# A 32-sample two-layer linear/softmax attention kernel: layer 0's query product as four full-array matmuls into one PSUM bank, and a new order of all pieces

## Chip, cores and metric

The kernel runs on one core of one Trainium2 chip. The metric is the device time of one execution in microseconds (us); lower is better. Times of one kernel in several runs agree within about 0.1%.

## What is computed

The reference takes x of shape (32, 256, 256) and a condition vector per sample, and applies two conditioned attention layers, one after the other. All 32 samples are independent. In short:

```
layer 0 (8 heads of 32):
  xn = ln(x);  q = softmax(xn @ Wq + bq, over the 32 features of a head)
  k  = softmax(xn @ Wk + bk + mask, over the 256 tokens);  v = (xn @ Wv + bv) * mask
  att = k^T v   (32 x 32 per head);   y = q @ att   (per head)
  x  = x + silu(ln(y) * (1 + scale) + shift) @ W_out + b_out
layer 1 (16 heads of 16):
  ordinary softmax(q k^T) v attention with the same wrapping
```

The change touches `y = q @ att` of layer 0, called the query product here. `att` is block-diagonal over heads: of a 128 x 128 block of features (four heads), only the four 32 x 32 blocks on the diagonal are not zero.

## The kernel before

The work of one sample ("batch" b) is cut into some 60 kinds of pieces, a function each, such as `k0(b)`, `y0(b)`, `rows(b, u)`. Each of the five queues (PE, DVE, ACT, POOL, and SP for DMA) has its pieces written out by hand in one fixed order: 1275 pieces on PE, 1025 on DVE, 884 on ACT, 740 on POOL and 398 on SP. Samples overlap: PE works on `k0` of sample 20 while `cols` of 13 and `pv` of 12 are under way. An engine takes its pieces strictly in the order of its list, so a piece whose input is late holds up what stands behind it. Every piece ends in an increment of a semaphore, on which its users wait.

PSUM has 8 banks. The table `BANK` gives each group of results (`gq0`, `gy0`, `gr3`, ...) a home bank for each sample, and the table `FREED` names what a piece must wait for before it may write there. Matmuls on 64-row halves of the array run in pairs into two neighbouring banks, `n` and `n + 1`; `n` is then even. That holds for `rows` and `cols` (layer 1's scores, each 128 x 1024), `ty`, the transposes `ktT`, `qtT`, `y0T`, `y1T`, and, before the change, `y0`.

The pieces around the change, for sample b: `att` (PE, L771) makes the 32 x 32 blocks; `at_` (ACT, L1712) copies them into the tile `AT`, which is zeroed once by a memset (L2131), so that what is off the diagonal stays zero; `qt` (ACT, L1702) fills `QTs`; `y0` (PE, L784) multiplies; `rq` (DVE, L1244) makes reciprocals of the softmax sums; `Y0` (DVE, L1259) scales the product into `Y`; `s1` (DVE, L1188) takes statistics; `n1` (ACT), `r1` and `yn0` (POOL, L1989) normalise; `y0T` (PE, L718) transposes. Before the change a matmul of `y0` covers two heads, 64 rows of the array, so `AT` is only 64 columns wide, and features of the even and the odd pairs of heads land in two different banks. `Y` holds them in that order, and `yn0` puts them right as it writes.

Before the pieces run as a pipeline there is a set-up: loads of weights (`ld_w0`, `ld_f0`, `ld_w1`, ...), scales derived from their maxima (`w0m`, `w0p`), biases folded with matmuls over the whole array (`bb0`, `bb1` L976 and L978, `row3` L965 and L967), the condition's product `fx0` (L1002) and its turning `fm0` (L1009), and splits of each weight into a high and a low part in fp16 (`wh_*`, `wl_*`). On SP, `z0T(b)` (L525) turns the normalised input of sample b for PE; `mbd0` (L650) writes out the mask rows, for which it waits on DVE's `mb0`.

fp32 operands are multiplied in two passes, so one fp32 matmul of the program is two records of the trace.

Of the kernel before, what the change touches and what calls it, by code (L numbers as in the profile page):

```python
# [29 lines left out]
    "gpm": "1",  # L30
    "gt_w0": "0",
    "ga_w0": "0",
    "gcnd": "2",
    "gbb1": "3",
    "grow3": "4",
    "gt_o0": "0",
    "gbb0": "5",
    "gfx0": "2",
    "gq0": "00107411307003666226230345451347",
    "gfm0": "1",  # L40
    "gk0": "25515623626142177267061266500466",
    "gv0": "34246532232453342672373552017557",
    "gt_f0": "1",
    "gkt": "66224040400000624004646204204622",
    "gqt": "62622460642604640446040222406004",
    "gat": "05300311721547046360624675464663",
    "ga_o0": "5",
    "gy0": "26260644062664226044242606002020",
    "ga_f0": "4",
    "grw": "0",  # L50
    "gt_w1": "1",
    "gy0T": "26666464424220640642622624200062",
    "ga_w1": "4",
    "gcol": "5",
    "go0": "31221232543347226263557464035354",
    "gt_b": "0",
    "ga_b": "0",
    "gbb2": "2",
    "gq1": "05703334432467473624461600242452",
    "gfx1": "1",  # L60
    "gk1": "74032224522573323734465711442453",
    "gfm1": "1",
    "gv1": "00073326407633312247747627634533",
    "gt_f1": "1",
    "gt_o1": "7",
    "gr0": "62640666660046044460000626666266",
    "gr1": "26406622042420402460420664600244",
    "gr2": "62240660406406460006204640242046",
    "gr3": "44660200622066066462204264666600",
    "gr4": "42622226400002604406600624002266",  # L70
    "gr5": "64242260404022404020202242606042",
    "gr6": "46004620622664406600226004620006",
    "gr7": "64660264402400600004242062406644",
    "ga_o1": "6",
    "gc0": "22646004044004260040040406004022",
    "gc1": "44400662600460460246224606600664",
    "ga_f1": "2",
    "gc2": "44046262024626242602460040026022",
    "gc3": "66440240246444206626224424664446",
    "gc4": "46602060602600262206204606200022",  # L80
    "gpv0": "13225522566372725565651352543201",
    "gc5": "42440266024424002246222404266066",
    "gpv1": "10604533672363434474740342452314",
    "gc6": "40260606424020260062024666624442",
    "gpv2": "06714521672272437545647223543415",
    "gc7": "20446244460420004002260400600226",
    "gpv3": "02305266532717037446757722422512",
    "gty": "04620062000044466064462002644644",
    "gy1T": "40666042444266640062604440660666",
    "go1": "23552057726271557471227354230111",  # L90
# [5 lines left out]
    "gpm": "-",  # L96
    "gt_w0": "hot",
    "ga_w0": "mx_w0",
    "gcnd": "-",
    "gbb1": "-",  # L100
    "grow3": "-",
    "gt_o0": "w0p",
    "gbb0": "-",
    "gfx0": "csT",
    "gq0": (
        "mx_o0 q1:1 mx_f0 perm qt:3 kt:5 Y0:5 at:7 qa:5 max:31 yt:11 yt:16 exp:41 exp:48 yt:28 yt:32 yt:35 Y0:16 "
        "max:102 at:19 st1:12 yt:54 yt:60 yt:64 st1:16 yt:71 yt:75 yt:79 Y0:27 max:190 exp:185 v:32 "),
    "gfm0": "mc",
    "gk0": (
        "fy0 bc0 at:2 mx_w1 bm Y0:4 max:2 exp:1 max:21 yt:8 yt:10 at:11 yt:19 yt:24 st1:6 vt:11 max:83 q1:18 Y0:17 "  # L110
        "yt:48 at:20 at:21 exp:120 yt:61 at:24 Y0:24 at:26 max:174 Y0:27 at:29 at:30 at:31 "),
    "gv0": (
        "bc1 p3 st0:1 w1p qt:3 kt:5 at:6 film1 exp:9 max:29 at:10 st0:9 yt:20 q1:14 x1:12 st1:7 st1:8 exp:84 Y0:17 "
        "max:110 st1:12 ka:18 st0:20 max:141 st1:16 st0:23 exp:153 max:174 yt:84 yt:88 exp:185 exp:191 "),
    "gt_f0": "f0m",
    "gkt": (
        "- qt:1 v:3+x1:1 bc2+at:3 v:4+ke:5 at:5+mx_f1 qt:6 yt:3+yt:2 max:25 q1:10+max:31 exp:26 exp:36 exp:45 qt:13 "
        "Y1:7 exp:68 max:91 qt:17 max:104 qt:19 exp:107 Y1:14 exp:125 exp:131 exp:137 exp:150 max:170 max:178 Y1:21 "
        "qt:29 Y1:23 exp:196 "),
    "gqt": (  # L120
        "kt:1 Y0:1 st0:2 Y0:3 qt:4 max:7 max:15 max:23 max:32 exp:27 Y1:4 max:57 Y1:6 max:72 exp:69 exp:73 Y1:10 "
        "exp:94 max:111 kt:21 max:128 Y1:15 max:144 exp:138 v:26+st0:23 exp:155 at:27+q1:28 exp:173 Y1:22 exp:187 "
        "st0:29 st1:24 "),
    "gat": (
        "q1:2 o0p kt:3 qa:1 vt:1 max:2 q1:7 kt:8 max:28 max:38 yt:15 yt:17 x1:10 Y0:13 max:75 exp:72 max:95 max:98 "
        "max:108 max:116 st1:13 st0:20 max:141 max:148 Y0:24 kt:26 yt:78 yt:83 yt:87 max:196 exp:191 Y0:31 "),
    "ga_o0": "ke:2",
    "gy0": (
        "ke:1+v:1 kt:2 kt:4 st0:3 kt:6 max:10 exp:7 max:27 max:36 exp:31 max:50 qt:12 max:68 max:74 max:84 exp:79 "
        "max:100 exp:95 max:115 exp:110 exp:119 max:138 exp:134 max:157 exp:149 exp:158 max:181 qt:28 exp:182 qt:30 "  # L130
        "max:211 max:218 "),
# [12 lines left out]
    "gt_b": "q1:4",
    "ga_b": "mx_b",
    "gbb2": "kt:3",
    "gq1": (
        "fcs v:6 max:8 vt:3 exp:9 x1:7 o:2 ka:8 ke:13 x1:11 exp:59 x1:13 vt:12 exp:84 exp:90 exp:98 ka:17 x1:19 "
        "at:22 ka:20 ka:21 ka:22 exp:153 x1:25 ke:29 x1:27 o:22 ka:28 ka:29 vt:29 ka:31 o:27 "),
    "gfx1": "x1:2",  # L150
    "gk1": (
        "q1:5 q1:6 vt:2 ke:8 x1:6 o:1 v:11 v:12 v:13 o:5 qa:11 o:7 o:8 vt:13 max:102 v:20 v:21 o:13 v:23 vt:19 q1:25 "
        "ke:26 ke:27 o:19 q1:29 exp:179 q1:31 exp:195 yt:100 qa:30 vt:30 vt:31 "),
    "gfm1": "fy1",
    "gv1": (
        "at:4 Y0:5 ka:3 max:21 v:10 yt:12 max:46 max:56 st0:11 st1:6 exp:63 q1:17 yt:40 yt:45 max:110 yt:52 yt:55 "
        "qa:19 at:23 yt:68 o:17 yt:76 ka:24 max:183 max:190 yt:92 ke:32 at:32 st1:25 yt:107 max:237 yt:115 "),
# [26 lines left out]
    "gr6": (
# [2068 lines left out]
```

## Time and profile before

| | |
|---|---|
| median of 3 runs | 807.55 us (807.45 to 808.08) |
| the profiled execution's own time | 807.33 us |
| its span, first to last instruction | 805.6 us |
| mean granted TensorE clock | 0.985 |
| instructions | 29123 |

The profiled execution took 1.73 us more than its span (807.33 - 805.6); that part is outside of all that the profile shows. Busy times are sums over the span of each engine's instructions. For PE they are read with care: ends of matmuls are modelled, and a short gap between two matmuls is covered by the first one's modelled tail. What PE could do in the time is better read from where matmuls start.

### The profile page before, as it was taken

The numbers are of one execution on the slowest core, as the hardware profiler recorded it, in microseconds if no ns is written. First come the engines' busy times: TensorE is split into PE (matmuls) and PEld (weight loads), VectorE is DVE, ScalarE is ACT, GpSimd is POOL, SyncE is SP. The second block draws the span as 40 slices with busy tenths as digits, with TensorE's granted clock in tenths as the row PEclk, the third lists the DMA queues.
The fourth block names the chain that finished last, engine by engine and source line by source line (L and its number), as shares of the span: only waits on it lengthen the run. The fifth ranks groups of instructions, "written<-read, shape, count | busy, mean of one in ns | idle before, by whom it ended". The sixth has DMA issues, their size and how long they took to land. (4 is left out here: it accounts for less than half of the span.)

```text
span 805.6 us, 29123 instructions
## 1 busy us (share of the span) xinstructions
PE 772.6 (96%) x10431; PEld 538.0 (67%) x10431; DVE 710.9 (88%) x1392; ACT 701.6 (87%) x1658; POOL 681.8 (85%) x1085
## 2 busy tenths in 40 slices
PE   7999889999999999999999999999999999999985
PEld 3575765777777677777677767777677776656542
DVE  7698899999999899998899889999889989989953
ACT  2266768899999999999999999999999999999995
POOL 7379998989999999998899998998989988897334
PEclk8799999999999999999999999999999999999998
DMA  6423544444443544355653445444544363354301
GB/s 179 91 48 80 139 115 117 103 104 121 101 125 95 126 110 105 88 146 100 126 127 92 132 89 123 111 109 89 143 115 120 72 119 91 85 148 115 110 20 53
DMA packets 149283, 86.22 MB, mean 107 GB/s; under 512 B 87404, under 2 KB 141802, under 8 KB 149130
## 3 DMA queue, kind: packets, MB, share of 16 engines
q1 hardware_dynamic: 149140, 84.36, 43.1%
q8 instruction: 84, 1.38, 0.8%
q14 instruction: 59, 0.48, 0.2%
HBM read 39.64 MB, written 25.80 MB: 81 GB/s over the span
## 5 line engine op out<-in xcount | busy, mean ns | idle before, releaser
L1301 DVE TENSOR_REDUCE NM<-banks 128x4 f32<-128x1024 f32 x256 | 306.7, 1213 | 23.3 <-PE banks L832 21.0
L1783 ACT ACTIVATE wraw<-banks 128x1024 f32<-128x1024 f32 x154 | 157.2, 1038 | 8.5 <-PE banks L845 7.7
L1985 POOL TENSOR_TENSOR rs<-ve,nhalf 128x2 f32<-128x2 f32 x128 | 89.8, 703 | 32.9 <-ACT ve L1656 31.7
L1783 ACT ACTIVATE PX<-banks 128x1024 f32<-128x1024 f32 x102 | 104.0, 1034 | 5.5 <-PE banks L845 4.6
L832 PE MATMUL banks<-SK,SQ 51*128 51x256 f16 x1024 | 96.1, 272 | 3.6 <-DMA SK<-scr 1.2
L701 PE MATMUL banks<-wo,SH 128*128 128x256 f16 x768 | 95.5, 274 | 4.2 <-POOL SH L2073 4.2
L845 PE MATMUL banks<-SQ,SK 53*128 53x256 f16 x1024 | 96.8, 272 | 1.7 <-DVE NM L1301 1.1
L701 PE MATMUL banks<-wv,ZT 128*128 128x256 f16 x768 | 95.3, 275 | 0.9 <-DVE un L1436 0.8
L2073 POOL TENSOR_TENSOR SH<-ST,SH 128x512 f16<-128x512 f32 x64 | 74.5, 1166 | 23.7 <-ACT SH L1747 20.0
L858 PE MATMUL banks<-wraw,V 128*32 128x256 f32 x1232 | 87.7, 385 | 0.7 <-ACT PX L1783 0.3
L2010 POOL TENSOR_TENSOR ZHL<-Z,ZHL 128x256 f16<-128x256 f32 x128 | 83.1, 670 | 2.6
L701 PEld LDWEIGHTS banks<-wo,SH 128*128 128x128 f16 x768 | 71.7, 98 | 19.9 <-POOL SH L2073 5.8
L701 PEld LDWEIGHTS banks<-wv,ZT 128*128 128x128 f16 x768 | 72.2, 98 | 16.0 <-issue 6.7
L2101 POOL TENSOR_TENSOR AB<-R,AB 128x512 f16<-128x512 f32 x64 | 74.6, 1172 | 6.5 <-ACT AB L1763 6.3
L1734 ACT ACTIVATE TH<-banks,hB,hA 128x256 f32<-128x256 f32 x128 | 65.6, 569 | 10.4 <-PE banks L718 7.9
L1989 POOL TENSOR_SCALAR Z<-X,nm,rs 128x256 f32<-128x256 f32 x128 | 69.7, 553 | 4.5 <-issue 2.2
L1989 POOL TENSOR_SCALAR YN<-Y,nm,rs 128x256 f32<-128x256 f32 x128 | 69.7, 553 | 2.4
L1763 ACT ACTIVATE R<-banks,fcs 128x256 f32<-128x256 f32 x128 | 62.7, 490 | 9.7 <-PE banks L709 8.8
L832 PEld LDWEIGHTS banks<-SK,SQ 51*128 51x128 f16 x1024 | 38.7, 95 | 42.4 <-issue 21.9
L845 PEld LDWEIGHTS banks<-SQ,SK 53*128 53x128 f16 x1024 | 37.9, 96 | 43.4 <-issue 21.3
L1737 ACT ACTIVATE banks<-banks,fB,fA 128x256 f32<-128x256 f32 x128 | 64.2, 550 | 0.0
L1763 ACT ACTIVATE AB<-banks,fcs 128x256 f16<-128x256 f32 x128 | 63.2, 494 | 0.0
(187 smaller groups left out, 1782.8 us busy)
## 6 DMA issues: line engine op xcount, KB each, us to landing
scr<-AB SPq DMA_DIRECT2D x64, 256.0 KB, 2.6
X<-in_x_dram SPq DMA_DIRECT2D x32, 256.0 KB, 3.0
SQ<-scr SPq DMA_DIRECT2D x64, 128.0 KB, 2.8
SK<-scr SPq DMA_DIRECT2D x64, 128.0 KB, 2.9
out_dram<-wemb SPq DMA_DIRECT2D x32, 256.0 KB, 2.6
SQ<-scr SPq DMA_DIRECT2D x64, 64.0 KB, 2.8
SK<-scr SPq DMA_DIRECT2D x64, 64.0 KB, 3.0
wemb<-in_L_cond_W_emb_dram SPq DMA_DIRECT2D x1, 1024.0 KB, 5.3
```

Source lines behind the costliest of these rows:

```text
L701: m = PE.matmul(dst[:, t, :], zt[:, j, k, t * P:(t + 1) * P], w[:, i, k, :], start=(k, n) == (0, 0), stop=(k, n) == (1, 2))
L832: m = PE.matmul(banks[:, n + j % 2, (j // 2) * T:(j // 2) * T + T], SQ[p, r, h, c * P:(c + 1) * P], SK[p, r, h, :], start=True, stop=True)
L845: m = PE.matmul(banks[:, n + j % 2, (j // 2) * T:(j // 2) * T + T], SK[p, r, h, c * P:(c + 1) * P], SQ[p, r, h, :], start=True, stop=True)
L858: m = PE.matmul(banks[32 * j:32 * j + 32, n, 0:T], V1[:, r, c, 4 * g + j, :], px((8 * b + u) % 5)[:, at_px(j):at_px(j) + T], start=(c == 0 ...
L1301: V.tensor_reduce(NMe[:, c, :, 2 * g:2 * g + 2], banks[:, n:n + 2, :].rearrange("p a (h m) -> p a h m", m=T), AX.X, ALU.max, negate=True). ...
L1763: t = A.activation(dst, bank(home(f"g{c}1", b))[:, f, :], ACT.Identity, bias=fcs[:, i, f:f + 1], scale=(r_q, r_k)[i])
L1783: A.activation(px(v % 5), banks[:, n:n + 2, :].rearrange("p a n -> p (a n)"), ACT.Exp, scale=r_uu).then_inc(S["exp"])
L1985: G.tensor_tensor(rs[:, b % 2, l, :], ve[:, b % 2, l, :], nhalf[:, :], ALU.pow).then_inc(S[f"r{l}"])
L1989: i = G.tensor_scalar(dst[:, t], src[:, t], nm[:, b % 2, l, t:t + 1], rs[:, b % 2, l, t:t + 1], ALU.add, ALU.mult)
L2010: i = G.tensor_tensor(ZHL[:, l, b % 2, 1, k], z[:, :, k, :], ZHL[:, l, b % 2, 0, k], ALU.subtract)
L2073: G.tensor_tensor(by_half(SH[:, l, 1]), ST[:, l].rearrange("p h (q j) -> p h q j", j=HALF), by_half(SH[:, l, 0]), ALU.subtract).then_inc(S ...
L2101: G.tensor_tensor(AB[:, i, :, 1], R1[:, i], AB[:, i, :, 0], ALU.subtract).then_inc(S["sp" + c])
```

## The change

`AT` becomes 128 columns wide, and `at_` puts each head's block on its own place on the diagonal. `y0` makes four matmuls, each of 128 rows, 128 columns of weights and 128 moving columns, in place of eight of 64 rows and 64 moving columns, and all four write one bank. `Y` is in natural order, and `rq`, `Y0`, `s1` and `yn0` lose their rearrangements. All five orders, and with them `BANK` and `FREED`, are new throughout; the pieces in them are the same, each once.

```
-        rqs = sb("rq", [P, 2, 2, 8])
+        rqs = sb("rq", [P, 2, 2 * 8])
-        AT = sb("AT", [P, 2, HALF])
+        AT = sb("AT", [P, 2, P])
...
-                        for h in range(2):
-                            r, q = slice(HALF * h, HALF * h + HALF), 2 * c + f
-                            m = PE.matmul(banks[:, n + h, q * HALF:(q + 1) * HALF], QTs[r, o, f, c * P:(c + 1) * P], AT[r, f, :],
-                                          start=True, stop=True)
+                        m = PE.matmul(bank(n)[:, c, f * P:(f + 1) * P], QTs[:, o, f, c * P:(c + 1) * P], AT[:, f, :],
+                                      start=True, stop=True)
...
-                V.reciprocal(rqs[:, b % 2].rearrange("p a (q h) -> p q a h", h=2), qsum[:, :].rearrange("p (q a h) -> p q a h", q=4, a=2)).then_inc(
-                    S["rq"])
+                V.reciprocal(rqs[:, b % 2], qsum[:, :]).then_inc(S["rq"])
...
-                V.tensor_tensor(Y[:, 0].rearrange("p a (q d) -> p a q d", d=32),
-                                banks[:, n:n + 2, 0:T].rearrange("p a (q d) -> p a q d", d=32),
-                                rqs[:, b % 2].unsqueeze(3).to_broadcast([P, 2, 8, 32]), ALU.mult).then_inc(S["Y0"])
+                V.tensor_tensor(heads(Y[:, 0]), banks[:, home("gy0", b), :].rearrange("p (h f) -> p h f", f=32),
+                                each(rqs[:, b % 2]), ALU.mult).then_inc(S["Y0"])
...
-                stats(b, 1, by_token(Y[:, 0]))
+                stats(b, 1, Y[:, 0])
...
-                    h, c = slice(32 * j, 32 * j + 32), slice(32 * (j % 2), 32 * (j % 2) + 32)
-                    i = A.activation(AT[h, :, c], banks[h, home("gat", b), 0:64].rearrange("p (f n) -> p f n", f=2), ACT.Identity)
+                    h = slice(32 * j, 32 * j + 32)
+                    i = A.activation(AT[h, :, h], banks[h, home("gat", b), 0:64].rearrange("p (f n) -> p f n", f=2), ACT.Identity)
...
-                apply(b, 1, natural(YN[:, 0], 64), split_rows(Y[:, 0], 64), "yn0")
+                apply(b, 1, YN[:, 0], Y[:, 0], "yn0")
```

The start of the SP and PE orders, and a stretch of the PE order from the middle, before (-) and after (+):

```
SP
-            ld_m(); x_in(0); ld_c(); ld_w0(); mbd0(); x_in(1); ld_o0(); x_in(2); ld_r(); ld_f0(); ld_w1(); am(0)
-            x_in(3); am(1); x_in(4); fd(); z0T(0); z0T(1); z0T(2); am(2); fill_q(); ...
+            x_in(0); ld_m(); ld_c(); ld_w0(); ld_o0(); x_in(1); ld_r(); ld_f0(); fd(); mbd0(); x_in(2); am(0)
+            x_in(3); z0T(0); x_in(4); fill_q(); am(1); z0T(1); ld_w1(); z0T(2); am(2); ...
PE
-            hot(); pm(); tr_w0(); ar_w0(); cnd_t(); bb1(); row3(); tr_o0(); bb0(); fx0(); q0(0); fm0(); k0(0); v0(0)
-            ... tr_b(); qtT(2); ktT(2); ar_b(); bb2(); att(2); v0(4); o0(1); ktT(3); q0(4); y0(2); q1p(0); fx1()
+            hot(); cnd_t(); pm(); tr_w0(); ar_w0(); row3(); bb0(); bb1(); fx0(); k0(0); fm0(); q0(0); v0(0); tr_o0()
+            ... tr_b(); bb2(); fx1(); qtT(2); ar_b(); att(2); q0(4); ktT(3); v0(4); o0(1); att(3); q1p(0); y0(2)
```

Counted over the whole lists, among the pieces of the samples: PE changes from a piece of one array shape to a piece of another (128 x 128: `k0 q0 v0 o0 q1p k1p v1p o1`; 64 x 128: `rows cols ty` and the transposes; 128 x 32: `pv att`) 608 times in the order before, with `y0` as 64 x 128, and 585 times in the order after, with `y0` as 128 x 128.

## Rows read from the trace of the kernel before

**Rows 1.** The page: span, and busy time of each engine (share of the span).
```profile
span 805.6 us, 29123 instructions
...
PE 772.6 (96%) x10431; PEld 538.0 (67%) x10431; DVE 710.9 (88%) x1392; ACT 701.6 (87%) x1658; POOL 681.8 (85%) x1085
```
**Rows 2.** Busy time in stretches: PE, PEld, DVE, ACT, POOL, clock, DMA share, GB/s.
```profile
16.00:20.00 4.00, 4.00 (x10) 1.52 (x8) 2.29 (x7) 2.33 (x7) 3.79 (x6) 0.50 0.83 240
...
40.00:60.00 20.00, 19.53 (x251) 14.68 (x249) 18.25 (x60) 12.62 (x42) 15.51 (x26) 1.00 0.21 49
60.00:80.00 20.00, 18.01 (x164) 11.65 (x163) 16.99 (x51) 13.84 (x40) 18.34 (x28) 0.91 0.32 81
...
100.00:740.00 640.00, 630.28 (x8908) 450.68 (x8908) 589.59 (x1092) 597.41 (x1409) 580.49 (x917) 1.00 0.46 111
300.00:400.00 100.00, 98.99 (x1407) 72.92 (x1406) 91.42 (x173) 94.92 (x228) 92.33 (x147) 1.00 0.51 116
500.00:600.00 100.00, 98.13 (x1419) 70.42 (x1418) 90.00 (x172) 93.65 (x223) 90.45 (x142) 1.00 0.47 109
```
**Rows 3.** Waits between 60 and 780 us: total, times, longest.
```profile
DVE NM L1301 <- PE banks L832: 21.0, 46, 1.1
...
DVE Y L1259 <- PE banks L784: 13.8, 20, 1.9
```
**Rows 4.** Instructions by line and shape: busy us, mean ns, idle before.
```profile
L784 PEld LDWEIGHTS banks<-AT,QT 64*128 64x128 f32 x512 | 31.4, 188 | 5.0 <-issue 4.6
...
L1259 DVE TENSOR_TENSOR Y<-banks,rq 128x512 f32<-128x512 f32 x32 | 22.0, 688 | 14.4 <-PE banks L784 14.2
L1314 DVE TENSOR_TENSOR Y<-banks,rd 128x512 f32<-128x512 f32 x32 | 21.9, 684 | 0.4
...
L1989 POOL TENSOR_SCALAR Z<-X,nm,rs 128x256 f32<-128x256 f32 x128 | 69.7, 553 | 4.5 <-issue 2.2
L1989 POOL TENSOR_SCALAR YN<-Y,nm,rs 128x256 f32<-128x256 f32 x128 | 69.7, 553 | 2.4
```
**Rows 5.** PE from 406 to 411 us: start, duration, instructions.
```profile
405.87 1.07 PE L858 MATMUL banks<-wraw,V 128*32 128x256 f32 x16
406.76 0.61 PE L858 MATMUL banks<-PX,V 128*32 128x256 f32 x8
...
409.50 0.39 PE L845 MATMUL banks<-SQ,SK 53*128 53x256 f16 x4
409.73 1.00 PE L784 MATMUL banks<-AT,QT 64*128 64x64 f32 x16
410.57 0.38 PE L832 MATMUL banks<-SK,SQ 51*128 51x256 f16 x4
410.88 0.46 PE L771 MATMUL banks<-V,KT 128*32 128x32 f32 x32
```
**Rows 6.** PE from 15 to 33 us, the set-up.
```profile
15.51 2.04 PE L976 MATMUL banks<-wraw,lnc 128*128 128x256 f32 x4 [1.10 <-issue]
...
18.63 1.87 PE L965 MATMUL banks<-wraw,lnc 128*3 128x256 f32 x4
...
24.53 6.38 PE L1002 MATMUL banks<-wemb,csT 128*32 128x512 f32 x8
30.84 1.48 PE L701 MATMUL banks<-wq,ZT 128*128 128x256 f16 x12
```
**Rows 7.** DVE from 3 to 36 us, the set-up.
```profile
2.95 0.39 DVE L1474 TENSOR_SCALAR SK<-SK 32x256 f32<-32x256 f32 x1 [1.50 <-DMA SK<-in_mask_BxS_ff_dram]
...
32.73 0.17 DVE L1412 TENSOR_SCALAR be1c<-bec 128x2 f32<-128x2 f32 x1 [5.38 <-PE banks L1009]
...
35.79 0.68 DVE L1218 TENSOR_REDUCE kmr<-banks 128x2 f32<-128x512 f32 x1
```
**Rows 8.** SP's queue: start, duration, instructions.
```profile
8.53 0.35 SPq L650 DMA_DIRECT2D mbd<-PX  x1
...
12.47 0.25 SPq L612 DMA_DIRECT2D SK<-in_L_cond_k_b_dram  x1
```

More of the change, by code:

```diff
@@ L47 @@
-    "ga_o0": "5",
[L48 to L53, printed above, removed]
+    "gcnd": "1",
+    "gpm": "0",
+    "gt_w0": "2",
+    "ga_w0": "2",
+    "grow3": "3",
+    "gbb0": "4",
+    "gbb1": "5",
+    "gfx0": "4",
+    "gk0": "55433734610414223406160050627650",
+    "gfm0": "4",
+    "gq0": "11244311360505467117075541700326",
+    "gv0": "34016525203125036456671423236720",
+    "gt_o0": "0",
@@ L84 @@
[L84 to L90, printed above, removed]
+    "gfx1": "0",
+    "ga_b": "1",
+    "gq1": "75303710644365020630453273261030",
+    "gk1": "53442600125270160700421362301051",
+    "gfm1": "4",
+    "gv1": "26077100032050706104423724110546",
@@ L91 @@
+    "gty": "04262260426444260640042246240044",
+    "gy1T": "24066000620642446260022266024022",
+    "go1": "61074326717171152006230014065111",
 }
@@ L252 @@
     "PE": (
-        "hot pm tr_w0 ar_w0 cnd bb1 row3 tr_o0 bb0 fx0 fm0 tr_f0 ar_o0 ar_f0 rw tr_w1 ar_w1 col tr_b ar_b bb2 fx1 "
+        "hot cnd pm tr_w0 ar_w0 row3 bb0 bb1 fx0 fm0 tr_o0 tr_f0 ar_o0 ar_f0 rw col tr_w1 ar_w1 tr_b bb2 fx1 ar_b "
         "fm1 tr_f1 tr_o1 ar_o1 ar_f1 ").split(),
     "DVE": (
-        "hz mb0 csl w0m mx_w0 o0m w0p p3 mx_o0 wl_q0 wl_k0 wl_v0 f0m mx_f0 o0p w1m film0 mx_w1 wl_o0 w1p bm mx_b fcs "
-        "wl_q1 wl_k1 wl_v1 f1m o1m mx_o1 mx_f1 o1p film1 wl_o1 ").split(),
+        "hz mb0 csl w0m mx_w0 o0m w0p p3 wl_k0 wl_q0 wl_v0 f0m mx_f0 mx_o0 o0p film0 wl_o0 w1m mx_w1 bm w1p wl_v1 "
+        "mx_b wl_q1 fcs wl_k1 f1m o1m mx_f1 mx_o1 o1p film1 wl_o1 ").split(),
     "ACT": (
-        "th pa csT wh_q0 wh_k0 wh_v0 bc0 bc1 mc fy0 perm wh_o0 wh_k1 bc2 wh_q1 wh_v1 fy1 wh_o1 ").split(),
+        "th pa csT bc0 wh_v0 wh_k0 bc1 wh_q0 fy0 mc wh_o0 perm wh_v1 wh_k1 wh_q1 bc2 fy1 wh_o1 ").split(),
     "POOL": (
-        "cst v1z nmz mb1 ").split(),
+        "cst nmz v1z mb1 ").split(),
 }
@@ L687, in _ @@
-            nw(27); wq(29); out_(24); nr(27); wk(29); rq6(29); z1T(30); rk6(29); nT(28); wk(30); nw(28); wq(30)
-            nr(28); rk6(30); rq6(30); z1T(31); nT(29); nw(29); out_(25); wk(31); nr(29); wq(31); rk6(31); rq6(31)
-            nT(30); out_(26); nw(30); nr(30); out_(27); nT(31); nw(31); nr(31); out_(28); out_(29); out_(30); out_(31)
+            x_in(0); ld_m(); ld_c(); ld_w0(); ld_o0(); x_in(1); ld_r(); ld_f0(); fd(); mbd0(); x_in(2); am(0); x_in(3)
+            z0T(0); x_in(4); fill_q(); am(1); z0T(1); ld_w1(); z0T(2); am(2); ld_o1(); ld_f1(); am(3); z0T(3); z0T(4)
@@ L1042, in col @@
                 t.then_inc(C["PE"])
-            hot(); pm(); tr_w0(); ar_w0(); cnd_t(); bb1(); row3(); tr_o0(); bb0(); fx0(); q0(0); fm0(); k0(0); v0(0)
-            tr_f0(); k0(1); q0(1); ktT(0); v0(1); qtT(0); att(0); q0(2); ar_o0(); ktT(1); y0(0); ar_f0(); att(1)
-            qtT(1); rw(); tr_w1(); k0(2); y0T(0); y0(1); ar_w1(); k0(3); q0(3); v0(2); col(); o0(0); y0T(1); v0(3)
-            k0(4); tr_b(); qtT(2); ktT(2); ar_b(); bb2(); att(2); v0(4); o0(1); ktT(3); q0(4); y0(2); q1p(0); fx1()
@@ L1173, in _ @@
-            pv(31, 6); pv(31, 7); y1T(30); ty(31); o1(29); y1T(31); o1(30); o1(31)
+            hot(); cnd_t(); pm(); tr_w0(); ar_w0(); row3(); bb0(); bb1(); fx0(); k0(0); fm0(); q0(0); v0(0); tr_o0()
+            k0(1); ktT(0); q0(1); v0(1); att(0); tr_f0(); qtT(0); q0(2); y0(0); k0(2); ar_o0(); qtT(1); ktT(1)
+            ar_f0(); rw(); att(1); y0T(0); v0(2); y0(1); col(); tr_w1(); k0(3); ar_w1(); ktT(2); q0(3); o0(0); v0(3)
+            y0T(1); tr_b(); bb2(); fx1(); qtT(2); ar_b(); att(2); q0(4); ktT(3); v0(4); o0(1); att(3); q1p(0); y0(2)
@@ new lines, in _ @@
+            cols(10, 7); y0(16); rows(12, 4); y0T(15); pv(10, 6); att(17); pv(10, 7); k0(18); rows(12, 5); y1T(9)
+            v0(18); cols(11, 0); q0(18); cols(11, 1); ty(10); rows(12, 6); k1p(14); q1p(14); cols(11, 2); ktT(18)
+            rows(12, 7); o1(9); v1p(13); rows(13, 0); cols(11, 3); pv(11, 0); pv(11, 1); cols(11, 4); cols(11, 5)
+            rows(13, 1); o0(15); cols(11, 6); qtT(17); rows(13, 2); pv(11, 2); pv(11, 3); pv(11, 4); pv(11, 5)
+            rows(13, 3); cols(11, 7); rows(13, 4); y0(17); att(18); pv(11, 6); pv(11, 7); rows(13, 5); y0T(16)
@@ new lines, in _ @@
+            att(23); pv(16, 4); pv(16, 5); pv(16, 6); pv(16, 7); rows(18, 5); cols(17, 0); v1p(19); k0(24)
+            rows(18, 6); y0T(21); ty(16); q0(24); v0(24); ktT(24); cols(17, 1); o1(15); rows(18, 7); cols(17, 2)
+            cols(17, 3); k1p(20); o0(21); cols(17, 4); qtT(23); rows(19, 0); q1p(20); rows(19, 1); cols(17, 5)
+            rows(19, 2); pv(17, 0); pv(17, 1); pv(17, 2); pv(17, 3); cols(17, 6); rows(19, 3); pv(17, 4); pv(17, 5)
+            rows(19, 4); y0T(22); cols(17, 7); y0(23); rows(19, 5); y1T(16); q0(25); k0(25); cols(18, 0); pv(17, 6)
@@ new lines, in _ @@
+            q1p(22); rows(21, 0); cols(19, 3); o1(17); k1p(22); rows(21, 1); rows(21, 2); cols(19, 4); o0(23)
+            pv(19, 0); cols(19, 5); rows(21, 3); cols(19, 6); pv(19, 1); pv(19, 2); pv(19, 3); cols(19, 7)
+            rows(21, 4); ktT(26); y0(25); rows(21, 5); y1T(18); y0T(24); q0(27); k0(27); att(26); pv(19, 4); pv(19, 5)
+            pv(19, 6); pv(19, 7); cols(20, 0); rows(21, 6); o1(18); v0(27); cols(20, 1); qtT(26); rows(21, 7); o0(24)
+            cols(20, 2); ty(19); cols(20, 3); k1p(23); rows(22, 0); ktT(27); cols(20, 4); q1p(23); v1p(22)
@@ new lines, in _ @@
+            rows(25, 6); v1p(26); cols(24, 1); rows(25, 7); o1(22); cols(24, 2); ty(23); cols(24, 3); k1p(27)
+            cols(24, 4); rows(26, 0); q1p(27); o0(28); rows(26, 1); ktT(31); pv(24, 0); pv(24, 1); rows(26, 2)
+            cols(24, 5); y0(30); cols(24, 6); rows(26, 3); pv(24, 2); pv(24, 3); cols(24, 7); rows(26, 4); y1T(23)
+            pv(24, 4); rows(26, 5); pv(24, 5); pv(24, 6); y0T(29); pv(24, 7); rows(26, 6); cols(25, 0); v1p(27)
+            att(31); rows(26, 7); ty(24); qtT(31); k1p(28); o1(23); cols(25, 1); cols(25, 2); rows(27, 0); q1p(28)
```

1055 lines of the change are left out of this document (510 added, 545 removed), and 8 rows, old and new, of the table FREED.

## The prediction, made before the changed kernel had been run

> **What bounds the kernel now.** I read the page first, for who is busy. No engine stands out: PE 96%, DVE 88%, ACT 87%, POOL 85% of the span [rows 1]. Then the stretches [rows 2], to see whether a mean hides stages. Between 100 and 740 us DVE is busy 589.59 of 640 us (92%), ACT 93%, POOL 91%, so all three are nearly full at once, and none of them waits for one fixed partner. Before 100 us and after 740 us they are not. So there are three places where time can go: the fill, the long middle and the drain. In the middle DVE idles 50.4 us (640 - 589.59), and that is what an order can win or lose. The waits [rows 3] tell who keeps DVE: 21.0 us behind `rows`, 46 times, and 13.8 us behind `y0`, 20 times, the product that is changed.
>
> PE's 99% is a number to distrust, so I took the starts of its matmuls [rows 5]. The eight matmuls of `y0` are 16 records in 409.73 to 410.57, 0.84 us. They run as pairs on the two halves of the array, so these are 8 slots of 0.105 us. `rows` and `cols` before and after it have the same shape; four of their matmuls, two slots, take 0.23 us (409.50 to 409.73). Where the next piece has another shape, as from `rows` to `att`, 410.57 to 410.88 is 0.31 us for the same two slots: about 0.09 us more. From `pv` to `pv`, 405.87 to 406.76, four slots of 256 moving fp32 columns take 0.89 us, 0.22 each. So a change of the array's shape costs PE some 0.09 us, and it happens 608 times in the order before: 55 us of PE's 772.6 that look busy and are not.
>
> **The change part by part.**
>
> *The product itself.* Four matmuls in two passes are again 8 slots, each with 128 moving columns, which by the 0.22 us for 256 is 0.11 us, if the weights of the next pass load meanwhile. 8 x 0.11 = 0.88 against 0.84 us: 0.04 x 32 = 1.3 us of PE more. If loads did not overlap, a slot would be 0.11 + 0.105 us; I take 0.105 as the load of 128 fp32 columns, since the slots of `y0` now, with only 64 moving columns, are as long as that, while a load itself shows 188 ns from end to end [rows 4]. That would be 1.72 us a sample, (1.72 - 0.84) x 32 = 28 us of PE. These are the two bounds. I take the lower. The set-up has the same kind of matmul, fp32 over the whole array: with 128 columns of weights four records took 2.04 us, and with 3 columns of weights 1.87 us, both at a granted clock of 0.50, which is 1.2 GHz [rows 2, 6]. An exposed load would add at least 0.21 us to each of the four at that clock (0.105 x 2), 0.84 us; the difference is 0.17.
>
> This is where a rule speaks against the change. The Trainium skill (TensorE: Matmul & The Clock Gate, Part 3, The mechanism) says that a weight load overlaps with matmuls in flight only when the row group differs, which a product over all rows can't have. By that rule the sum below would be some 28 us higher. By that rule the set-up's matmuls would have been longer too, and the trace does not agree with it there.
>
> *Changes of shape.* `y0` was of the shape of `rows` and `cols`, between which it mostly stands; it is now of the projections' shape. The new order has 585 changes in place of 608: 23 x 0.09 = -2.1 us of PE. With the 1.3 us above PE comes out at -0.8 us, which is nothing: 0 in the sum.
>
> *ACT, DVE, POOL.* `at_` copies four blocks of the same size as before. `rq` and `s1` have the same elements. `Y0` reads 512 elements a partition from one bank in place of two: 688 ns now; `Y1_`, the same operation on two banks with another stride, takes 684 ns [rows 4], so the form does not matter within 4 ns, 0.1 us over 32. `yn0` loses a rearrangement in POOL: its instructions take 553 ns, and those of `Z`, which has none, 553 ns [rows 4]. All zero. Were any of them dearer, the cover is thin (DVE idles 8% of the middle): 50 ns on 32 instructions would be 1.6 us at most.
>
> *The wider memset of AT* runs on POOL in the first 6 us, before POOL has its first input; zero.
>
> *The bank.* One bank less is held from the start of `y0` to the end of `Y0`, and `y0` need not find an even pair free. This can only help, if the order uses it: the nearest row is DVE's 13.8 us behind `y0`. The bounds are 0 and 13.8 us.
>
> *The set-up, where the new order can be followed.* SP sends `mbd0` behind `ld_f0` now. In the run before it stopped SP until 8.53 us, and what stood behind it, `ld_o0`, `x_in(1)`, the bias rows and the condition's weights, went out from 9 us on, the last bias row at 12.47 [rows 8]. These now go some 3 us sooner. PE's first bias product began at 15.51 after a wait of 1.10 us [rows 6]; that wait goes. Against this, `x_in(0)` now goes ahead of the masks, and DVE began with the mask at 2.95 us [rows 7] and had no gap after that until the maxima; I let it start 0.5 us later. Net: PE reaches `fx0` 0.6 to 1 us sooner. `fx0`, 6.3 us from its start to the next, at the low clock, is ahead of the first projection in both orders [rows 6]. The first projection is then `k0(0)` and not `q0(0)`; DVE, which had waited 5.38 us for `fm0` until 32.73 and took `km(0)` at 35.79 [rows 7], gets `km(0)` as soon as `k0(0)` ends, near 31.7. So DVE resumes 1.0 us sooner: -1.0 us, bounds +0.5 (masks late, nothing gained) and -2. `ld_w1` is moved behind `z0T(1)`, whose input is ready at about 23 us; behind it in SP's queue stands `z0T(2)`, for which POOL is not ready until 30 us, so its five DMAs (some 4.5 us of SP) delay nobody, and DVE needs the weights only past 45 us.
>
> *The fill, 40 to 80 us.* DVE idles 1.75 + 3.01 = 4.8 us, and the clock falls to 0.91 in 60 to 80 us [rows 2], where PE had little to do between `tr_b` and `ar_b`. The new order puts `bb2` and `fx1` there. I take -1.0 us; bounds 0 and -4.
>
> *The middle.* -1.0 us for the bank: 2% of DVE's idle 50.4 us. This is a choice, not a sum; the bounds are the two rivals below. *The drain:* past the last `rows` the five lists hold the same pieces in nearly the same order; 0.
>
> Sum: 0 + 0 - 1.0 - 1.0 - 1.0 = -3.0 us. The profiled execution took 807.33 us (span 805.6 and 1.73 around it), 0.22 below the median. 807.33 - 3.0 = 804.3, and by the median 804.5 us, 0.4% faster.
>
> **The rivals.**
> A, *the wait for y0 goes for good*: half of the 13.8 us besides the fill's gain: 807.55 - 2 - 7 = 798.5 us. For it: it is DVE's second largest wait, and DVE is nearly full. Against it: what DVE does not wait for here it may wait for at the next `rows`, since ACT is busy 93% and POOL 91% [rows 2].
> B, *nothing comes of it*: the order before was as good as this machine allows, and the gain in the set-up is taken back at the first `rows` that waits for DMA or POOL: 807.5 us. For it: three engines above 90%.
> C, *the new order waits more in the middle* (the other side). Place: DVE's queue, behind `rows` and `y0`. Within the kernel before the same pieces leave DVE idle 8.6 us in one stretch of 100 us and 10.0 in another [rows 2]; so 1 us per 100 is what the place in the pattern alone can do. 640 us at 1 us per 100 worse is +6.4, less 2 from the fill: 812 us. It decides from 0.3 us per 100 upward.
> D, *the weights' load is not hidden*: 28 us of PE, of which PE's own gaps take a few: 807.5 + 24 - 3, some 829 us. Only this one would be plain from one number, the starts of the matmuls behind `y0`.
>
> **Chances.** The forecast (a gain of 1.6 to 7 us) 0.47, A 0.10, B 0.19, C 0.20, D 0.04. Faster by over 0.2% (that is 1.6 us, about what a measurement of this kernel can tell from no change): 0.57; within 0.2%: 0.19; slower: 0.24. The range goes from A to C, 798.5 to 812 us, and leaves D and the ends out. The forecast's own range is 801 to 806.
>
> **What would show it.** In the profile after: `y0` at 0.88 to 0.90 us from its first start to the next piece's, plus 0.09 where the shape changes (D: 1.7). `Y0` at 660 to 690 ns, `yn0` at 553. The first projection at about 30 us, and DVE back at work by 32. DVE's wait for `y0` below 13 us. DVE's idle time in 100 to 740 us below 50 us; above 53 it is C. The prediction is wrong if the set-up's gain is there and the middle eats it, or if `y0`, now among pieces of another shape, comes later to DVE than before.

## The result, and the profile after

The changed kernel takes 802.55 us (median of 6 runs, 800.37 to 804.89), the kernel before 808.29 us (6 runs, 807.45 to 808.76): the ratio is 0.9928, interval 0.9902 to 0.9954. That is 5.7 us faster. Timed a second time it came to 802.02 us, ratio 0.9924 (0.9901 to 0.9948). I had forecast a gain of 3 us in a range (801 to 806 us) that holds this time. The times of one kernel lie further apart than the 0.1% that three runs had shown: in the second timing the kernel before was run 23 times, from 806.16 to 812.21 us, and the changed kernel 6 times, from 800.43 to 805.37. So differences of a few tenths of a per cent are read below from medians of many runs, and not from one.

The profiled execution took 804.03 us. The page, as [rows 1]:

```profile
span 802.3 us, 28619 instructions
...
PE 773.3 (96%) x10175; PEld 543.1 (68%) x10175; DVE 709.5 (88%) x1392; ACT 700.7 (87%) x1658; POOL 681.4 (85%) x1085
```

256 records of matmuls fewer (32 samples by 8), and every engine is as busy as before within 1.4 us. Two executions of the kernel before differ by more than that on DVE (710.9 and 714.1 us in the run "Before again" below), so no engine's work got measurably cheaper, and the gain has to be looked for in idle time. The stretches, as [rows 2]:

```profile
16.00:20.00 4.00, 4.00 (x9) 1.64 (x8) 3.73 (x11) 0.66 (x2) 3.68 (x7) 0.50 0.23 70
...
40.00:60.00 20.00, 19.96 (x213) 15.02 (x214) 18.91 (x63) 12.70 (x42) 16.69 (x26) 1.00 0.35 85
60.00:80.00 20.00, 19.87 (x214) 13.94 (x214) 19.48 (x58) 14.07 (x41) 18.85 (x28) 1.00 0.21 44
80.00:100.00 20.00, 15.43 (x199) 11.36 (x196) 16.09 (x49) 15.20 (x49) 18.73 (x30) 0.91 0.48 123
100.00:740.00 640.00, 634.39 (x8714) 458.14 (x8716) 591.75 (x1094) 598.45 (x1409) 581.28 (x920) 1.00 0.46 112
```

In 40 to 80 us DVE's idle time falls from 4.76 to 1.61 us and the clock no longer drops in 60 to 80 us; a dip of the same size (0.91) now lies in 80 to 100. There DVE idles 3.91 us where it idled 2.62 before, so part of what 40 to 80 us win is given back: over 40 to 100 us DVE's idle time falls from 7.38 to 5.52 us. In 100 to 740 us DVE idles 48.25 us, 2.2 less than [rows 2].

DVE's waits between 130 and 740 us, with `y0` behind the fill (total, times, longest):

```profile
DVE NM L1297 <- PE banks L831: 21.4, 51, 1.0
DVE ST L1267 <- ACT banks L1732: 4.5, 13, 0.8
DVE Q L1228 <- PE banks L702: 3.1, 4, 1.4
...
DVE Y L1256 <- PE banks L783: 1.7, 6, 0.3
```

and the same stretch of the kernel before:

```profile
DVE NM L1301 <- PE banks L832: 19.4, 41, 1.1
DVE Y L1259 <- PE banks L784: 10.2, 17, 1.3
...
DVE ST L1271 <- ACT banks L1737: 1.8, 4, 0.6
...
DVE Q L1229 <- PE banks L701: 0.8, 2, 0.4
```

This pair is the one to learn from. The wait for `y0` fell by 8.5 us, and DVE's idle time in the same stretch by 1.8 (busy 562.07 us in place of 560.27). The rest came back under other names: 2.0 us more behind `rows`, 2.7 behind ACT's tanh and scaling of the transposed product (`ST`), 2.3 behind the query's projection. A wait that goes is not a gain until one has seen what the engine waits for next.

The instructions of the changed pieces, as [rows 4]:

```profile
L783 PEld LDWEIGHTS banks<-AT,QT 128*128 128x128 f32 x256 | 31.0, 191 | 6.5 <-issue 6.3
...
L1256 DVE TENSOR_TENSOR Y<-banks,rq 128x512 f32<-128x512 f32 x32 | 21.9, 684 | 2.3 <-PE banks L783 1.7 <-POOL YN L1983 0.2
...
L1983 POOL TENSOR_SCALAR YN<-Y,nm,rs 128x256 f32<-128x256 f32 x128 | 69.8, 554 | 2.2
```

PE around one `y0`, as [rows 5]:

```profile
407.59 0.38 PE L831 MATMUL banks<-SK,SQ 51*128 51x256 f16 x4
407.90 1.16 PE L783 MATMUL banks<-AT,QT 128*128 128x128 f32 x8
409.00 0.39 PE L831 MATMUL banks<-SK,SQ 51*128 51x256 f16 x4
409.32 0.46 PE L772 MATMUL banks<-V,KT 128*32 128x32 f32 x32
```

From its first start to the next piece `y0` takes 1.10 us, not 0.97 to 0.99. By the starts of the eight records the first slot is 0.214, the next six 0.112 each, and the last, with the change of shape, 0.208. That is the same in most of the 32; where `y0` stands behind a projection, whose shape it shares, the first slot is 0.11 to 0.13 us. The median of the whole is 1.09 us, and 34.2 us are spent in all against 29.6 in the kernel before.

The set-up, PE and then DVE, as [rows 6, 7]:

```profile
14.41 0.54 PE L894 MATMUL banks<-mxd,ones 3*128 3x3 f32 x2 [3.03 <-DVE mxd L1333]
14.88 1.87 PE L964 MATMUL banks<-wraw,lnc 128*3 128x256 f32 x4
...
17.62 2.07 PE L975 MATMUL banks<-wraw,lnc 128*128 128x256 f32 x4
...
23.92 5.67 PE L1001 MATMUL banks<-wemb,csT 128*32 128x512 f32 x8
29.52 0.83 PE L734 MATMUL banks<-ZT,wk 128*128 128x256 f16 x6
```

```profile
4.71 0.28 DVE L1470 TENSOR_SCALAR SK<-SK 32x256 f32<-32x256 f32 x1 [3.26 <-DMA SK<-in_mask_BxS_ff_dram]
...
31.27 0.69 DVE L1217 TENSOR_REDUCE kmr<-banks 128x2 f32<-128x512 f32 x1 [4.15 <-PE banks L736]
```

The first projection at 29.5 us and DVE back by 31.3 us are where I had put them. PE's first bias product (now `row3`) starts at 14.88 in place of 15.51 us and `fx0` at 23.92 in place of 24.53, 0.6 us sooner, as I had it. The way there was another. The wait of 1.10 us ahead of the bias products is gone, but one of 3.03 us for the maxima's product stands ahead of them now. DVE's mask work began 1.8 us later, not 0.5, and DVE then waited 2.03 us for the second sample's input, which stands in its list ahead of the maxima:

```profile
13.08 0.75 DVE L1187 BATCH_NORM_STATS2 st<-X 128x6 f32<-128x256 f32 x2 [2.03 <-DMA X<-in_x_dram]
```

To see where the gain is made I compare two profiled executions of each kernel by the ends of the same four instructions (the second of the kernel before is the experiment "Before again" below). `Y0` of the first sample ends the set-up, the last maximum of sample 1 the fill, that of sample 31 the middle, the last output row the drain:

```
us                         before       before again  after        after again
to Y0(0)                   45.08        43.59         43.58        40.93
Y0(0) to maxima(1)         85.63        86.34         84.61        84.65
maxima(1) to maxima(31)    641.25       642.76        639.73       640.24
maxima(31) to output(31)   31.00        31.62         31.74        31.78
```

The means differ by -2.1, -1.4, -2.0 and +0.5 us, together -5.0. No one place made the gain. With two profiles of each kernel these are rough: the set-up alone differs by 1.5 us between the two of the kernel before and by 2.65 between the two of the changed one.

### The profile page after: what moved, and what is told of

It reads as the page before. It is cut to its first block and busy times, and to the rows that moved or that the text cites. A ratio compares the mean times of both kernels' runs of the same rounds, so it can differ in the third digit from the quotient of the medians.

```text
span 802.3 us, 28619 instructions
## 1 busy us (share of the span) xinstructions
PE 773.3 (96%) x10175; PEld 543.1 (68%) x10175; DVE 709.5 (88%) x1392; ACT 700.7 (87%) x1658; POOL 681.4 (85%) x1085
## 5 line engine op out<-in xcount | busy, mean ns | idle before, releaser
L844 PE MATMUL banks<-SQ,SK 53*128 53x256 f16 x1024 | 94.4, 272 | 2.4 <-ACT wraw L1778 1.5
```

The costliest lines, as they stand in the source:

```text
L844: m = PE.matmul(banks[:, n + j % 2, (j // 2) * T:(j // 2) * T + T], SK[p, r, h, c * P:(c + 1) * P], SQ[p, r, h, :], start=True, stop=True)
```

## The experiments

Besides the changed kernel's second timing there are eleven. Each is the changed kernel with the edit shown, unless it says otherwise; the times are medians, the ratio is to the kernel before on the same chip.

**The product without the order.** The kernel before with its own orders and banks and only the new product (all edits of the change that don't touch an order), the second bank freed.

> The kernel before, with its five orders and its home banks, and only the new product: four full-array matmuls into the one bank n, natural order in Y; what waited for bank n+1 because of the product no longer does. PE changes shape 652 times in place of 608 (+44 x 0.09 = +4.0 us of PE), and the product costs 0.04 us more a sample (+1.3). Theory 1 (the gain is in the order, the product is neutral): 807.5 to 813 us, ratio 1.000 to 1.007. Theory 2 (the freed bank gives the gain by itself): 803 to 806, ratio below 0.998. Theory 3 (weights of a full-array product load in the open): some 28 us more, 830.

Measured: 811.97 us (12 runs), ratio 1.0035 (1.0019 to 1.0050), slower by 0.35%. DVE's waits between 60 and 780 us:

```profile
DVE NM L1298 <- PE banks L832: 20.8, 50, 1.3
DVE Y L1257 <- PE banks L784: 16.4, 21, 1.6
```

The wait for `y0` grew from 13.8 us [rows 3] to 16.4. The product is dearer (34.4 us for 32, against 29.6), and an order that was written for a pair of banks has no use for the one that is free. So none of the gain comes from the product by itself; it came with the new order. Whether a new order for the old product, with its pair of banks, would have gained as much was not tried.

**The pair held.** For 23 of the 32 samples (all but 1 to 5, 7, 12, 25 and 27) `y0` waits for the second bank of the pair too and keeps it; product and orders stay.

```
 "gy0": (
-    "mx_f0 perm kt:4 v:5 vt:1 qt:6 max:18 max:27 max:37 max:43 max:49 x1:10 exp:56 exp:62 ...
+    "mx_f0+q1:3 perm kt:4 v:5 vt:1 qt:6 max:18+yt:3 max:27 max:37 max:43+yt:14 max:49 x1:10+yt:21 exp:56 ...
```

> The changed kernel, but for 23 of the 32 samples the product waits for its bank's partner too, and the partner's next user waits for Y0, as if it still took a pair. Nothing else differs. Theory 1: the order hardly uses the freed bank, 0 to +2 us against the changed kernel. Theory 2: the gain goes, +4 us or more, ratio to the kernel before 0.998 or above.

Measured: 846.97 us, ratio 1.0468 (1.0447 to 1.0489). From maxima(1) to maxima(31) it takes 685.26 us in place of 640. Between 60 and 780 us:

```profile
DVE NM L1299 <- PE banks L833: 50.6, 68, 3.7
...
PE banks L785 <- ACT wemb L1788: 13.8, 9, 2.7
```

So the new order leans on the free bank all along: without it, it is 45 us worse than with it, and 38 us worse than the kernel before. This is no price of the bank by itself (an order written for the pair does without it, at 808 us); it shows that this order was made for one bank, so that product and order can't be priced apart and added.

**The fill's pieces put back.** On PE `bb2` goes behind `ar_b` and `fx1` behind `y0(2)`, on ACT `fy1` behind `qa(0)`.

```
-tr_b(); bb2(); fx1(); qtT(2); ar_b(); att(2); ... y0(2)
+tr_b(); qtT(2); ar_b(); bb2(); att(2); ... y0(2); fx1()
```

> The changed kernel with bb2 and fx1 put back on PE behind ar_b and behind the third sample's product, and fy1 put back on ACT behind qa(0), as in the kernel before. Theory 1 (half or more of the gain is made between 60 and 80 us, where these two fill PE's gap): +1.5 to +3 us against the changed kernel, and the granted clock falls again before 80 us. Theory 2: within 0.5 us of the changed kernel.

Measured: 810.62 us (12 runs), ratio 1.0016 (1.0000 to 1.0033): 8.6 us more than the changed kernel, and its whole gain gone. That is far above either theory. PE around `ar_b`, and the stretch:

```profile
61.52 0.69 PE L720 MATMUL banks<-ident,QE 64*128 64x64 f32 x8 [2.98 <-DVE ST L1268]
63.98 0.58 PE L895 MATMUL banks<-mxd,ones 2*128 2x2 f32 x2 [1.77 <-DVE mxd L1334]
64.49 2.08 PE L976 MATMUL banks<-wraw,lnc 128*128 128x256 f32 x4
...
68.24 2.74 PE L703 MATMUL banks<-wq,ZT 128*128 128x256 f16 x12
```

```profile
60.00:80.00 20.00, 16.71 (x152) 10.77 (x152) 13.26 (x40) 10.07 (x29) 17.40 (x27) 0.74 0.20 43
```

PE waits 2.98 and 1.77 us, and its matmuls run at the low clock (1.2 GHz) from the first of these waits until 71 us (twelve of the projection's take 2.74 us, 1.48 at the full clock). Y0(0) to maxima(1) takes 92.39 us in place of 84.6; the middle behind it takes 640.3, as ever. My own edit brought most of that: the kernel before has these pieces there too and pays only 1.4 us, presumably because the rest of its order is made for it. It does show that in this order the two pieces (with `fy1`) keep PE busy and the clock up here; what they are worth in the changed kernel it does not tell.

**SP's start.** Once the changed kernel with SP's order of before up to `z0T(4)`, once the kernel before with SP's order of after.

```
-x_in(0); ld_m(); ld_c(); ld_w0(); ld_o0(); x_in(1); ld_r(); ld_f0(); fd(); mbd0(); x_in(2); am(0); x_in(3)
+ld_m(); x_in(0); ld_c(); ld_w0(); mbd0(); x_in(1); ld_o0(); x_in(2); ld_r(); ld_f0(); ld_w1(); am(0); x_in(3)
```

> The changed kernel with SP's start in the order of the kernel before (masks first, mbd0 ahead of ld_o0, ld_w1 ahead of the first z0T), all else new. Theory 1, which has the set-up's 1.3 us come from SP's order: +1 to +2 us. Rival: what SP's start gives it takes back by the later mask (DVE begins at 4.71 in place of 2.95 us) and by x_in(1), for which DVE waits 2.0 us: within 0.7 us either way.

> The kernel before with SP's start in the order of the changed kernel, all else old. Theory 1: -0.5 to -2 us. Rival: 0, or up to 1 us slower, since DVE's mask work stands ahead of everything on DVE's queue and the masks come 1.8 us later.

Measured: 801.80 us, ratio 0.9917 (0.9892 to 0.9943), and 809.68 us, ratio 1.0010 (0.9993 to 1.0027). SP's order is worth nothing that can be measured, from either side. My reason for the set-up's gain is refuted. In the profile of the kernel before with the new SP order the wait ahead of the bias products is gone, but DVE's masks come 1.1 us later than [rows 7], and the maxima with them:

```profile
4.09 0.43 DVE L1474 TENSOR_SCALAR SK<-SK 32x256 f32<-32x256 f32 x1 [2.64 <-DMA SK<-in_mask_BxS_ff_dram]
```

```profile
14.07 0.42 PE L895 MATMUL banks<-mxd,ones 3*128 3x3 f32 x2 [0.93 <-DVE mxd L1337]
...
14.89 2.08 PE L976 MATMUL banks<-wraw,lnc 128*128 128x256 f32 x4
```

The maxima's product started at 13.38 us in both profiles of the kernel before; its first bias product started at 15.51 us in one and at 14.52 in the other.

**Key and query of the first sample put back.**

```
-fx0(); k0(0); fm0(); q0(0)       PE
+fx0(); q0(0); fm0(); k0(0)
-km(0); f0m(); q1(0)              DVE
+f0m(); q1(0); km(0)
```

> The changed kernel, but TensorE runs q0(0) ahead of k0(0) again and VectorE f0m and q1(0) ahead of km(0), as before; all else of the new order stays. Theory one (the lead of the set-up comes from taking the key's half of the first sample ahead of the query's, since VectorE could take km(0) at 31.3 us and not at 35.8 us): Y0(0) ends 1.5 to 3 us later than in the changed kernel, and if the lead is kept through the middle as it was in the other runs, the time is 804 to 805 us, ratio 0.995 to 0.997. Theory two (the lead comes from the rest, the condition's product and row3 ahead of the weights' row work on TensorE, and the masks): the time stays at 801 to 803 us, ratio 0.991 to 0.994.

Measured: 805.13 us (12 runs, 802.09 to 807.73), ratio 0.9956 (0.9940 to 0.9972). By the ratios some 2.5 us of the gain go, by the medians about 3; the intervals overlap a little (0.9940 to 0.9972 here, 0.9901 to 0.9948 for the changed kernel). The profiled execution was the fastest of the twelve, so it can't show where these are lost. In it the clock held until 28 us, which it did in neither profile of the changed kernel, and still `Y0(0)` ended at 42.03. `km(0)` began at 27.75 us; in the mended start below, where PE reached `fx0` at the same time (17.92 us, here 17.90), it began at 23.74. What the clock had won was lost here:

```profile
25.59 1.47 PE L703 MATMUL banks<-wv,ZT 128*128 128x256 f16 x12
30.23 0.37 PE L889 MATMUL banks<-ident,mxw 128*1 128x128 f32 x1 [3.16 <-ACT mcol L1820]
30.39 1.48 PE L735 MATMUL banks<-ZT,wk 128*128 128x256 f16 x6
```

PE idles 3.16 us and then takes 1.48 us for what takes 0.83 at the full clock. That `km(0)` comes sooner with the key first is shown; that `Y0(0)` does because of it can't be told apart from the clock in these profiles.

**The product twice.** Every matmul of `y0` is made twice, the second time over the first.

> The changed kernel with every query product done twice over into the same bank (the second overwrites the first with the same numbers). It prices PE time in the middle: the eight slots more should take 0.85 to 0.9 us a sample, 28 us of PE. If PE is a full bound, +25 to +28 us. If PE still has slack that the busy share hides, +8 to +18 us. If the weights' load were in the open, each product would take 1.7 us and this one twice that.

Measured: 824.31 us, ratio 1.0181 (1.0155 to 1.0207). 8 x 0.112 x 32 = 28.7 us of PE cost about 22 us, 0.77 us per us, between the two forecasts. That is not the price of PE's time alone, since the second set of matmuls also delays `Y0`: between 60 and 780 us DVE waits for `y0`

```profile
DVE Y L1255 <- PE banks L782: 15.0, 16, 1.2
```

in place of 1.7 us in the changed kernel.

**Before again.**

> The kernel before once more, as a second profiled execution beside the first. Theory one (the changed kernel's lead is made ahead of 130 us, and what a kernel's set-up takes moves between executions): the ratio to itself is 1.000 within 0.2 %, the last row of the first sample's y0 ends at 44 to 46 us, and max(1) to max(31) takes 640.5 to 642 us, about 1 us above the 639.7 and 640.2 us of the changed kernel. Theory two (the middle itself moves by several us between executions, so that no lead of 1 us can be read in it): that stretch differs from the first profile's 641.3 us by over 2 us.

Measured: 809.33 us (10 runs), ratio to itself 1.0008 (0.9993 to 1.0023). The set-up moved by 1.5 us between two executions, and the middle by 1.5 (641.25 and 642.76), and in the one profile with SP's new order it took 645.17, so the kernel before can differ in its middle by several us. The new order's middle stays within 638.4 to 640.3 in eight executions with different starts. So it is faster there in all of them, by about 1 us at least (641.25 - 640.30); how much more can't be told from single executions.

**The start, mended.** Three versions. The first puts the masks first on SP, `x_in(1)` ahead of `ld_o0`, and on DVE `mx_w0` ahead of `s0(1)`:

```
-x_in(0); ld_m(); ld_c(); ld_w0(); ld_o0(); x_in(1)      SP
+ld_m(); x_in(0); ld_c(); ld_w0(); x_in(1); ld_o0()
-w0m(); s0(1); mx_w0(); o0m()                            DVE
+w0m(); mx_w0(); s0(1); o0m()
```

> The changed kernel with three edits to its start: masks ahead of x_in(0), x_in(1) ahead of ld_o0, and mx_w0 ahead of s0(1) on DVE, so that PE does not wait for DVE (3.03 us before ar_w0 in the changed kernel). PE's first bias product should start at 12.5 to 13 us in place of 14.88 and the first projection 1.5 to 2 us sooner. If the set-up's lead survives to the end, as theory 1 has it: -1 to -2 us against the changed kernel. If it is taken back at the first piece that waits for something else: 0.

Measured: 800.75 us (798.92 to 804.72), ratio 0.9904 (0.9877 to 0.9931). The best profiled execution of all, with the clock at full speed through the set-up:

```profile
12.79 0.35 PE L894 MATMUL banks<-mxd,ones 3*128 3x3 f32 x2 [1.64 <-DVE mxd L1333]
...
14.55 1.13 PE L975 MATMUL banks<-wraw,lnc 128*128 128x256 f32 x4
...
17.92 3.62 PE L1001 MATMUL banks<-wemb,csT 128*32 128x512 f32 x8
22.00 0.83 PE L734 MATMUL banks<-ZT,wk 128*128 128x256 f16 x6 [0.46 <-DVE wq L1388]
...
28.38 0.27 PE L888 MATMUL banks<-ident,mxw 128*1 128x128 f32 x1 [1.58 <-ACT mcol L1819]
30.55 0.83 PE L734 MATMUL banks<-ZT,wk 128*128 128x256 f16 x6 [1.91 <-DMA ZT<-ZHL]
```

The first projection starts at 22.0 us, 7.5 sooner than in the changed kernel's first profile, and `Y0(0)` ends at 39.61, only 4.0 sooner: two new waits, 1.58 us for ACT and 1.91 for a transfer, take the rest. The second version takes those two away: `mc` ahead of `n0(2)` on ACT, `z0(1)` ahead of `xb0(1)` on POOL, `am(1); z0T(1)` ahead of `x_in(4)` on SP.

> The mended start (masks' operands loaded first, the second sample's rows ahead of the output weights' on SP, mx_w0 ahead of s0(1) on VectorE), and besides mc ahead of n0(2) and ke(0) on ScalarE, z0(1) ahead of xb0(1) on GpSimd and z0T(1) with am(1) ahead of x_in(4) on SP, which take away TensorE's waits of 1.58 us for mcol and 1.91 us for the second sample's transposed input. Theory one (the lead that the first 50 us make is kept to the end): Y0(1) ends 2 us or more before the 48.7 us of the mended start, and the time is 797 to 800 us, ratio 0.986 to 0.990. Theory two (by then VectorE's own queue sets the fill, PE's waits only move behind it): 800 to 802 us, ratio 0.990 to 0.992.

Measured: 802.79 us (797.10 to 803.99), ratio 0.9923 (0.9894 to 0.9952). It shows nothing either way. The waits are gone, but in the profiled execution the clock fell at 13 us, `L1002` took 5.76 us again, and the first projection came at 28.19. One run of six was the fastest of this whole study. The third version is the first with five idle matmuls more in PE's wait for the maxima:

```
-tr_w0(); ar_w0(); row3()
+tr_w0(); more_hot(); ar_w0(); row3()        more_hot: 5 matmuls of AB, 128x128 by 128x512, into bank 6
```

> The mended start with five more products of the warm-up's kind (128x128 by 128x512 in f16, their result unused, some 0.28 us each) on TensorE between the transposition of the three maxima and the product that spreads them, where it waited 1.64 us for mxd. Theory one (the spread of the changed kernel's times comes from whether the granted clock falls to half at 12 to 16 us, and it falls there because TensorE has idled for some 2 us): the clock stays at 1.00 from 10 to 32 us, Y0(0) ends by 40 us, the median is 798 to 799.5 us and no run is above 801 us. Theory two (the fall has to do with the length of the start and not with that gap): the clock still falls in part of the runs, the median is 800 to 802 us and the times spread over 4 us or more, as they did without the five.

Measured: 800.98 us (799.23 to 801.93), ratio 0.9895 (0.9874 to 0.9916). The clock stayed at 1.00 from 10 to 28 us, and the six times spread over 2.7 us, where the mended start's spread over 5.8; six are few to build on. The median did not fall, so neither theory came out whole. In the profiled execution:

```profile
12.29 0.27 PE L888 MATMUL banks<-ident,mxw 128*3 128x128 f32 x1 [2.18 <-DVE mxw L1372]
12.40 1.24 PE L961 MATMUL banks<-AB 128*128 128x512 f16 x5
...
29.05 0.27 PE L888 MATMUL banks<-ident,mxw 128*1 128x128 f32 x1 [1.66 <-ACT mcol L1824]
31.16 1.11 PE L734 MATMUL banks<-ZT,wk 128*128 128x256 f16 x6 [1.84 <-DMA ZT<-ZHL]
```

The maxima's transposition came 1.4 us later than in the mended start's profile, ahead of the five and not because of them, and behind the two later waits the clock fell to 0.63 in 32 to 36 us. This and the mended start are the fastest by their medians; their intervals overlap with the changed kernel's, so neither is shown to beat it.

## Why the prediction was right, and where not

*The product* was mis-sized. I had 0.88 us a sample and PE at -0.8 us together with the changes of shape. The slots are 0.112 as predicted, but the first of each `y0` is 0.21: 34.2 - 29.6 = +4.6 us of PE, of which I had counted 1.3, and the way out by the changes of shape. Alone it costs 0.35%. Rival D may have had the right idea for one load in eight: the extra 0.10 us of the first slot behind a change of shape is what a load in the open would look like (my estimate of one was 0.105), though no run proves that it is the load; the other seven are hidden. At 1.7 us a sample D is refuted, and so are the 55 us (1.72 x 32) that it would give for the product made twice. The Trainium skill (TensorE: Matmul & The Clock Gate, Part 3, The mechanism) has a load overlap with matmuls in flight only when the row group differs. The trace does not agree for seven loads of eight, with slots of 0.112 us over all rows. The same section also has a load into the background weight buffer pulled ahead of matmuls in flight, and with that statement the slots agree.

*ACT, DVE, POOL:* zero, as predicted (684 and 554 ns).

*The set-up* was predicted at -1.0 us and came to -2.1, and here the step that failed is "SP sends `mbd0` behind `ld_f0` now": the last bias row's DMA indeed went out at 8.4 us in place of 12.5, and the wait ahead of the bias products went with it, but SP's order is worth nothing in the time, from either side. Two things in the step were mis-sized. The wait was 1.10 us in one profile of the kernel before and 0.51 in the other, and I had only the first. And "I let it start 0.5 us later" was 1.1 to 1.8 us for DVE's masks, which stand ahead of the maxima that PE waits for; in the changed kernel a wait of 2.03 us for the second sample's input came on top. The other half of the step, `km(0)` as soon as `k0(0)` ends, came as I had it (31.27 us, predicted 31.7); undoing it costs 2.5 to 3 us, more than the whole set-up by my sum, though no profile shows where. What the other pieces that were moved on PE ahead of the projections do was not tried by itself. The bounds, +0.5 to -2, were too narrow for another reason: between two executions of one kernel the set-up moves by 1.5 to 2.65 us with the stretch in which the clock is low, and I had only one.

*The fill*, -1.0, came to -1.4, in part by the mechanism named: PE has `bb2` and `fx1` between `tr_b` and `ar_b`, and its waits there are gone. The clock was not won: it stays up until 80 us, but its dip comes in 80 to 100 us, as deep as before (0.91), in both profiles of the changed kernel.

*The middle*, -1.0, came to -2.0, with 1 us of uncertainty, in spite of 4.6 us more of PE. Of rival A half came true: the wait for `y0` went for good (DVE's idle time ahead of `Y0` fell from 14.4 to 2.3 us in all). What it would give did not, for the reason I gave against it: between 130 and 740 us other waits, those for `rows`, for ACT and for a projection above all, took 6.7 of 8.5 us back. B is refuted in 6 of 6 runs, C in every profile, since the middle was shorter in each. The term was called "a choice", and that was honest; but "this can only help, if the order uses it" missed how far an order comes to depend on it (45 us). That the free bank is what shortened the middle is argued and not shown: the order changed throughout with it, and no run has a new order without the new product.

*The drain:* 0 predicted, +0.5 measured.

So the direction held, and the gain lies in the three stages where I had put it, but they came to -5.5 us and not -3.0 (set-up and middle to twice their size, the fill to 1.4 times), and the set-up's cause was wrong in one half. That the total still fell in the forecast's range is partly luck: two of the three terms were choices within wide bounds, and in the sum the price of the product was too low and the set-up and the middle too small.

## What to carry to other kernels

When a product gives back a resource, price the product in the old order and the new order as one thing: here the product alone was a loss of 0.35%, and the gain came with an order that can't stand without the free bank. Read the wait that vanishes together with the engine's idle time of the same stretch; 8.5 us of the one were 1.8 us of the other. A gap on TensorE can cost twice: waits of 2.98 and 3.16 us were followed by matmuls at the low clock. And a set-up is not read from one profiled execution, when two of the same kernel lie 1.5 to 2.65 us apart.

## What the runs showed of the hardware

*The first weights behind a change of shape.* A change between array shapes costs PE 0.09 to 0.10 us between starts (0.205 in place of 0.109 from 128 x 128 to 64 x 128, 0.199 in place of 0.105 the other way). With fp32 weights of 128 columns, here those of `y0`, the first slot of the new shape is longer by another 0.10 us in most cases (0.213, then 0.112), while behind a projection, which has the same shape, it is 0.11 to 0.13. The projections' own fp16 weights show it far less (0.120, then 0.109).

*The clock in the start.* In 16 to 20 us the granted clock was either 0.50 or 1.00, which is 1.2 or 2.4 GHz, and the times of one kernel spread more than the middle did in its profiles: the changed kernel's twelve times lie between 800.4 and 805.4 us, and its middle took 639.7 and 640.2 in the two profiles. In 11 of 14 profiled executions the clock was at half from 12 to 16 us until 24 to 30 us; PE's longest wait between 10 us and that point was 1.25 to 3.03 us. In three it held, behind longest waits of 1.62, 1.64 and 2.18 us. The lengths overlap, so the length of the wait does not decide alone. What else does, these runs don't show.

*What stays open.* 0.77 us per us of PE is measured by adding work to each `y0`, which makes DVE wait for it too. By that figure the 4.6 us that `y0` grew by would be 3.5 us, an estimate; whether a `y0` with a shorter first slot would win them was not tried. Nor was a new order for the old product, which alone could say how much of the 5.7 us needs the free bank.
